# GpSimd's row scatters one stage later and its key scaling ahead of the first addition, in a gated delta-rule layer with a mixture of experts

## The chip, the cores and the metric

One core of a Trainium2 chip runs the whole program. The metric is the device time of one execution in microseconds (us). Three runs of the kernel before took 1393.51, 1395.70 and 1396.22 us; the median is 1395.7.

## The reference

Input is x of 2 sequences of 2048 tokens with 128 channels. What is computed:

```
h    = layernorm(x)
q, k, v = causal depthwise convolution of 4 taps over (h @ qkv_w.T)      8 heads of 128
beta, alpha = gates of h, one number per head and token
for each token t and head:  S = alpha_t * S
                            S = S + k_t (beta_t * (v_t - k_t S))
                            o_t = q_t S
x    = x + (rmsnorm(o) * norm_w * silu(h @ z_w.T)) @ out_w.T
h    = layernorm(x)
x    = x + sum over the 2 best of 8 experts of  weight * (relu(h @ W1 + b1) @ W2 + b2)
```

## The kernel before, in words

The 4096 tokens are cut into 16 groups of two chunks of 128 tokens. The recurrence is computed chunk by chunk: within a chunk a triangular system of 128 rows per head is solved, and a state S of 128 x 128 per head is carried from chunk to chunk.

The work is a software pipeline over the groups. A call `stages(g, a, par)` on every engine does three things interleaved: it prepares group a = g + 1 (projections, convolution, decays, the triangular solve), it finishes group g (the recurrence, the norm, the output product), and it routes group r = g - 1 to the experts (layernorm, the router's logits, the two best experts, a destination row for each token, and scatters of the rows to memory). There are 17 such stages: `stages(None, 0)`, `stages(0, 1)`, ... `stages(14, 15)`, `stages(15, None)`. Behind them the last group is routed by itself, and then 39 tiles of 256 rows go through the experts.

The order of the steps in a stage is written out by hand in one string, `ORDER` (lines 249 to 265). Every engine walks through the same list and issues, in that order, what is its own. An engine never goes ahead of its own next instruction, so the order of a step matters on the engine that has it, and there alone.

The steps that the change and the prediction touch:

- GpSimd (lines 587 to 659) has these steps in a stage: `diag.c` (line 629, the decay matrix of chunk c before its scan, beta on the diagonal), `last.n` (line 637, 16 of them, the last addition of the convolution of one 128-channel tile; 0 to 7 are the keys, 8 to 15 the queries), `ka.c` (line 620, the keys of group g scaled by their decay), `aq.c` (line 620, the same for the queries), `sp.c` (line 649, the state scaled), `nr` (lines 589 to 600, the normalised rows of group r are written into `rowbuf`) and `sc` (lines 601 to 611, four indirect DMAs that scatter `rowbuf` to the rows that `dest` names, in the memory tensor `rows_in`).
- `sc` waits for `dest` (VectorE, line 1132) and for `rowbuf`. `nr` of the next group waits for the landing of all earlier scatters, since it overwrites `rowbuf`, and for `rs` (VectorE, line 237, step `rms`).
- `diag.c` waits for the attention product of the same chunk of the group before (`at`, VectorE line 1170), which still reads the decay matrix. `last.n` waits for `first.n`, the two multiply-adds of VectorE (lines 1143 and 1146), which wait for `taps.n` of ScalarE (line 758), which waits for `proj.n` of TensorE and for `last.n-4`: the convolution has a ring of 4 buffers.
- `ka.c` waits for the decays' transfer, asked for in the stage before, and for the attention matrix `kq.c.1` of TensorE, which still reads the unscaled keys. TensorE's `ks.c` reads the scaled keys.
- TensorE's `kk.0.1` and `kk.1.u` (line 1553) need all 8 key tiles, so `last.7`. Their products (VectorE, `nm`, line 1162) go to memory (line 477), come back as 32 x 32 blocks (line 485, tile `blkN`), and are solved on VectorE by `inv.0` to `inv.21`: pairs of a product with two SBUF inputs (line 1056) and a reduction (line 1060), between them other steps of the stage. The solved blocks go out and in again (`to`, `ti`) and are merged by TensorE in the next stage.
- In `ORDER` the string begins with `... m.0.0 last.0 taps.3 ... first.3 ka.0 last.1 ...` and ends with `... g.1.0 last.15 kd.1.0 inv.13 rms.0 ... nr ... ps ... st.1.1 xs.1 tj sc`. Of GpSimd's steps the order is: `diag.0 last.0 ka.0 last.1 last.2 last.3 diag.1 last.4` to `last.7 sp.0 aq.0 ... ka.1 ... sp.1 last.15 nr sc`.

Of the kernel before, what the change touches and what calls it, by code (L numbers as in the profile page):

```python
# [6 lines left out]
def preln_delta_moe_kernel(nc, x_in, qkv_t, z_t, ab_t, conv_w, dt_bias, a_log, norm_w, out_t,  # L7
# [11 lines left out]
    NG = NCH // GC  # L19
# [27 lines left out]
    with ctx:  # L47
        ctx.enter_context(nc.allow_non_contiguous_dma("layout of blocks"))

        def sb(name, shape, dt=F32):  # L50
            return ctx.enter_context(nc.sbuf_tensor(name, shape, dt))
# [20 lines left out]
        taps = sb("taps", [128, NT, TAPS])  # L72
# [6 lines left out]
        kq = sb("kq", [128, 2, 2, H, GT])  # L79
# [7 lines left out]
        def part(i, k):  # L87
            n = GC * H * C
            return area[i][:, n * k:n * k + n].rearrange("p (g h c) -> p g h c", g=GC, h=H)
# [4 lines left out]
        kd = part(2, 0)  # L94
        squares, spare = part(2, 1)[:, 0], part(2, 1)[:, 1]
        R, zg = part(3, 0), part(3, 1)
# [13 lines left out]
        rhs = sb("rhs", [128, H, C])  # L110
# [116 lines left out]
        def rsqrt_step(s, v, y, t):  # L227
# [19 lines left out]
        RMS = 1 + RSQ  # L247
        RMS_PART = (0, 6, RMS)
        ORDER = """
            proj.0 proj.1 taps.0 taps.1 diag.0 first.0 v.0.0 proj.2 m.1.0 taps.2 al.0 first.1 proj.3 m.0.0 last.0 taps.3  # L250
            rdiag.0 me.1.0 v.0.1 first.2 proj.4 first.3 ka.0 last.1 me.0.0 m.1.1 taps.4 proj.5 me.1.1 ks.0.0 m.0.1 taps.5
            scan.0 first.4 m.1.2 proj.6 me.0.1 rdiag.1 ks.0.1 last.2 last.3 first.5 me.1.2 proj.7 m.0.2 m.1.3 al.1 taps.6
            diag.1 first.6 taps.7 last.4 proj.8 first.7 kk.0.0 me.0.2 me.1.3 m.0.3 last.5 proj.9 last.6 xl.0 rhs.0.0 me.0.3
            last.7 sp.0 scan.1 nm.0.0 taps.8 kk.0.1 u.0.0 taps.9 aq.0 nm.0.1 kk.1.0 first.8 last.8 nm.1.0 kk.1.1 nm.1.1
            proj.10 ue.0.0 rhs.0.1 taps.10 o.0.0 first.9 proj.11 first.10 proj.12 u.0.1 taps.11 first.11 taps.12 last.9
            sd.0.0 proj.13 ktr.0.0 ue.0.1 first.12 xl.1 aq.1 last.10 no.0 no.1 sq.0.0 proj.14 taps.13 last.11 st.0.0 ac.0
            sd.0.1 taps.14 g.0.0 o.0.1 first.13 ka.1 st.0.1 sq.0.1 proj.15 last.12 v.1.0 sm v.1.1 scale.0 bi ks.1.0 kd.0.0
            first.14 inv.0 taps.15 ks.1.1 last.13 rhs.1.0 inv.1 inv.2 last.14 inv.3 inv.4 first.15 rhs.1.1 u.1.0 inv.5
            kq.0.0 u.1.1 ue.1.0 g.0.1 inv.6 ue.1.1 o.1.0 o.1.1 ktr.0.1 sq.1.0 inv.7 s2 ac.1 sd.1.0 sp.1 sq.1.1 kd.0.1 inv.8
            scale.1 inv.9 inv.10 at.0.0 inv.11 ktr.1.0 inv.12 g.1.0 last.15 kd.1.0 inv.13 rms.0 inv.14 sd.1.1 ktr.1.1 kd.1.1  # L260
            rms.1 gn.0.0 kq.0.1 gn.0.1 gt.0.0 inv.15 at.0.1 z.0.0 inv.16 gt.0.1 gte.0.0 nr g.1.1 xt inv.17 gte.0.1 z.0.1
            zt.0.0 xe lg out.0 gn.1.0 zt.0.1 inv.18 rk gn.1.1 gt.1.0 inv.19 gt.1.1 x2.0 inv.20 gte.1.0 inv.21 kq.1.0 gte.1.1
            pf out.1 zg.0.0 z.1.0 tp zt.1.0 zg.0.1 ps st.1.0 z.1.1 zt.1.1 zg.1.0 zg.1.1 xs.0 x2.1 to at.1.0 kq.1.1 at.1.1 ti
            st.1.1 xs.1 tj sc
            """
        STEPS = [(name, *map(int, arg)) for name, *arg in (word.split(".") for word in ORDER.split())]

        def halves(b, c, u):

            return (b + 1) * HALVES + U * c + u + 1  # L270

        def chunks(b, c):

            return (b + 1) * GC + c + 1
# [5 lines left out]
        def tile(b, n):  # L280

            return (b + 1) * NT + n + 1
# [62 lines left out]
        def bc(ap, shape):  # L345
            return ap.to_broadcast(shape)
# [210 lines left out]
        def _(pool):  # L557
# [55 lines left out]
            def stages(g, a, par):  # L613

                def scale_by_decay(c, kind, done):

                    pool.wait_ge(acum_in[c], g * 16 + 16)
                    pool.wait_ge(kq_ready, halves(g, c, U - 1))
                    t = kq[:, 1 - par, kind, :, C * c:C * c + C]
                    nc.gpsimd.tensor_tensor(t, t, acum_b[:, c, :, :], ALU.mult).then_inc(done, 1)  # L620

                r = g - 1 if g is not None and not (isinstance(g, int) and g == 0) else None
                for step, *arg in STEPS:
                    if r is not None:
                        route(step, r, par)
                    if step == "diag" and a is not None:
                        c, = arg
                        pool.wait_ge(at_ready, halves(a, c, U - 1) - HALVES)
                        nc.gpsimd.tensor_tensor(  # L629
                            decay[:, c, :, :], bc(ident[:, :].rearrange("p (o c) -> p o c", o=1), [128, H, C]),  # L630
                            bc(beta[:, ds(a * GC + c, 1), :].rearrange("p o (h u) -> p (o h) u", u=1), [128, H, C]),
                            ALU.mult).then_inc(diag_ready, 1)
                    elif step == "last" and a is not None:
                        n, = arg
                        dst = (kT[par], qT[par])[n // H]
                        pool.wait_ge(conv_mid, tile(a, n))
                        nc.gpsimd.tensor_tensor(dst[:, n % H, :], tapA[:, n % RING, :], tapB[:, n % RING, :],  # L637
                                                ALU.add).then_inc(conv_done, 1)
                    elif step == "ka" and g is not None:
                        scale_by_decay(arg[0], 0, ka_ready)  # L640
                    elif step == "aq" and g is not None:
                        scale_by_decay(arg[0], 1, aq_ready)
                    elif step == "sp" and g is not None:

                        c, = arg
                        pool.wait_ge(scale_ready, chunks(g, c))
                        pool.wait_ge(S_ready, halves(g, c, U - 1) - U)
                        pool.wait_ge(o_mm, halves(g, c, U - 1) - U)
                        nc.gpsimd.tensor_tensor(S[:, 1 - c, :, :], S[:, c, :, :],
                                                bc(a_end[:, c, :].rearrange("p (h o) -> p h o", o=1), [128, H, C]),  # L650
                                                ALU.mult).then_inc(sp_ready, 1)

            stages(None, 0, 0)
            stages(0, 1, 1)
            for b in range(1, NG - 1):
                stages(b, b + 1, 1 - b % 2)
            stages(NG - 1, None, 0)
            for step in ROUTE_ORDER:
                route(step, NG - 1, 1)

# [1125 lines left out]
```

## Time and profile before

| | |
|---|---|
| median of 3 runs | 1395.7 us |
| the profiled execution | 1399.73 us, of it 1397.9 us span |
| busy share TensorE, VectorE, ScalarE, GpSimd | 86%, 83%, 60%, 51% |
| mean granted clock of TensorE | 0.965 of full speed |
| scatters of line 609 | 64, 64.6 us busy |
| GpSimd's idle time ahead of them | 202.1 us, of it 175.2 us until VectorE's `dest` |

The profile is of one execution. A span runs from the first to the last instruction. An instruction's row gives its start, its duration and, in brackets, the idle time of its engine before it with what ended that. Rows with xN merge N instructions in a row. The chain of waits follows the run back from its last instruction, at each step to what released it.

### The profile page before, as it was taken

How to read it: one execution, taken by the hardware profiler on the slowest of the kernel's cores; microseconds unless marked ns; L12 is line 12 of the kernel's file. 1: busy time of each engine (PE TensorE's matmuls, PEld its weight loads, DVE VectorE, ACT ScalarE, POOL GpSimd, SP SyncE). 2: the span in 40 equal slices, each digit the busy share in tenths (PEclk: the TensorE clock that was granted, in tenths of full speed). 3: DMA queues.
4: the chain of work that ended last, by engine and by line, in shares of the span. 5: the costliest groups of instructions: out<-in, count | busy, mean ns of one | idle time of the engine just before them, and what ended most of it. 6: DMA issues, size and time to landing. Idle time of an engine off the chain costs nothing.

```text
span 1397.9 us, 34191 instructions
## 1 busy us (share of the span) xinstructions
PE 1199.9 (86%) x12203; PEld 944.0 (68%) x12203; DVE 1164.4 (83%) x2531; ACT 832.0 (60%) x2536; POOL 707.9 (51%) x598
## 2 busy tenths in 40 slices
PE   0355999999999999999999999999999989479991
PEld 0233868686868687777777777777777767358881
DVE  6878898989898998989898989897989783578875
ACT  1252666666666666657566666756566655358884
POOL 3151727464555656473828292928192822235552
PEclk9997999999999999999999999999999998789996
DMA  6031212222221222131313141313121223432225
GB/s 208 0 98 32 73 35 73 47 69 62 54 63 53 62 54 64 52 68 48 84 34 91 28 98 25 103 28 88 30 85 43 73 55 98 104 96 78 76 65 181
DMA packets 163176, 97.10 MB, mean 69 GB/s; under 512 B 115623, under 2 KB 148269, under 8 KB 161988
## 3 DMA queue, kind: packets, MB, share of 16 engines
q1 hardware_dynamic: 124932, 82.25, 21.6%
q10 hardware_dynamic: 33536, 4.20, 2.1%
q0 software_dynamic: 4544, 8.47, 1.9%
q8 instruction: 102, 1.67, 0.5%
q14 instruction: 62, 0.51, 0.1%
HBM read 73.31 MB, written 24.61 MB: 70 GB/s over the span
## 4 chain that ended last, share of the span: by engine, by line
DVE 37%; PE 21%; POOL 17%; issue 10%; DMA 9%; SPq 3%; ACT 3%; POOLq 0%; DVEq 0%; ACTq 0%
DVE blkT L1060 9%; POOL kq L637 9%; DVE Y_sb L1056 9%; DMA blkN<-scr_n 4%; PE kx L1553 3%; POOL decay L629 3%; POOL rows_in L609 2%; DVE Gs L1204 2%; POOL kq L620 2%; DMA scr_n<-area 2%; PE rc L1717 2%; SPq L477 2%; DVE blkN L1047 1%; DVE area L1170 1%; DVE Y_sb L1043 1%
## 5 line engine op out<-in xcount | busy, mean ns | idle before, releaser
L637 POOL TENSOR_TENSOR kq<-tapA,area 128x256 f32<-128x256 f32 x256 | 252.0, 998 | 93.6 <-DVE area L1146 92.8
L758 ACT ACTIVATE area<-pj,taps 128x256 f32<-128x256 f32 x256 | 123.1, 481 | 142.7 <-PE pj L1567 136.5
L1056 DVE TENSOR_TENSOR Y_sb<-blkT,blkN 128x4 f32<-128x4 f32 (+18 forms) x304 | 169.5, 558 | 10.5
L609 POOL DMA_INDIRECT rows_in<-rowbuf,dest x64 | 64.6, 1009 | 202.1 <-DVE dest L1132 175.2
L1143 DVE SCALAR_TENSOR_TENSOR tapA<-pj,taps,tapA 128x256 f32<-128x256 f32 x256 | 122.2, 477 | 53.4 <-ACT tapA L758 51.6
L1553 PE MATMUL kx<-kq 128*128 128x128 f32 x1024 | 141.0, 285 | 20.0 <-ACT area L767 9.6
L1553 PEld LDWEIGHTS kx<-kq 128*128 128x128 f32 x1024 | 128.7, 197 | 38.4 <-issue 21.8
L620 POOL TENSOR_TENSOR kq<-kq,area 128x1024 f32<-128x1024 f32 x64 | 151.1, 2362 | 0.0
L1060 DVE TENSOR_REDUCE blkT<-Y_sb 128x2 f32<-128x4 f32 (+18 forms) x304 | 142.4, 469 | 5.2
L758 ACT ACTIVATE tapA<-pj,taps 128x256 f32<-128x256 f32 x256 | 123.0, 480 | 0.0
L1146 DVE SCALAR_TENSOR_TENSOR area<-pj,taps,area 128x256 f32<-128x256 f32 x256 | 121.4, 474 | 0.0
L666 POOL DMA_INDIRECT rows_out<-rhs,e_dst x78 | 78.1, 1001 | 69.7 <-DVE e_dst L1325 36.7
L594 POOL TENSOR_TENSOR rowbuf<-rowbuf,id_step 128x4 int32<-128x4 int32 x16 | 3.2, 198 | 201.5 <-DVE rs L237 198.5
L1640 PE MATMUL ob<-S,kq 128*128 128x128 f32 x512 | 101.7, 281 | 0.8 <-issue 0.7
L1641 PE MATMUL ob<-Us,area 128*128 128x128 f32 x512 | 100.0, 277 | 0.0
L836 ACT ACTIVATE Gs<-Gs,rs 128x128 f32<-128x128 f32 x256 | 79.9, 397 | 32.3 <-DVE rs L237 32.3
L1603 PE MATMUL rc<-w_hi,xn_hi 128*128 128x512 f16 x256 | 99.1, 387 | 0.0
L1604 PE MATMUL rc<-w_lo,xn_hi 128*128 128x512 f16 x256 | 98.8, 386 | 0.0
L1605 PE MATMUL rc<-w_hi,xn_lo 128*128 128x512 f16 x256 | 98.7, 385 | 0.0
L1154 DVE TENSOR_TENSOR_SCAN decay<-area,decay 128x1024 f32<-128x1024 f32 x32 | 93.0, 2906 | 0.0
L629 POOL TENSOR_TENSOR decay<-ident,beta 128x1024 f32<-128x1024 f32 x32 | 60.8, 1901 | 62.3 <-DVE w_lo L1012 35.0
L827 ACT ACTIVATE area<-ob 128x128 f32<-128x128 f32 x256 | 67.7, 288 | 40.6 <-PE ob L1641 40.6
(307 smaller groups left out, 3613.2 us busy)
## 6 DMA issues: line engine op xcount, KB each, us to landing
area<-scr_alpha SPq DMA_DIRECT2D x32, 512.0 KB, 4.2
area<-scr_acum SPq DMA_DIRECT2D x32, 512.0 KB, 4.0
blkN<-scr_n SPq DMA_DIRECT2D x32, 256.0 KB, 4.4
area<-rows_in SPq DMA_DIRECT2D x39, 130.0 KB, 2.3
scr_n<-area SPq DMA_DIRECT2D x128, 32.0 KB, 1.6
area<-rows_out SPq DMA_DIRECT2D x4, 1024.0 KB, 8.1
rows_in<-rows_in SPq DMA_DIRECT2D x8, 260.0 KB, 3.8
kq<-in_x SPq DMA_DIRECT2D x4, 512.0 KB, 6.2
```

The lines of the kernel that those rows point to most:

```text
L620: nc.gpsimd.tensor_tensor(t, t, acum_b[:, c, :, :], ALU.mult).then_inc(done, 1)
L629: nc.gpsimd.tensor_tensor(decay[:, c, :, :], bc(ident[:, :].rearrange("p (o c) -> p o c", o=1), [128, H, C]), bc(beta[:, ds(a * GC + c, 1) ...
L637: nc.gpsimd.tensor_tensor(dst[:, n % H, :], tapA[:, n % RING, :], tapB[:, n % RING, :], ALU.add).then_inc(conv_done, 1)
L758: ins = nc.scalar.activation(dst[:, n % RING, :], pj[n % 2][:, k:k + GT], ACT.Copy, scale=taps[:, t, k:k + 1])
L1056: ins = nc.vector.tensor_tensor(p4, bc(blkT[:, r0:, j:].rearrange("p r (o m) -> p r o m", o=1), [128, nr, w, wd]), bc(blkN[:, j:j + w, j:] ...
L1060: ins = nc.vector.tensor_reduce(blkT[:, r0:, j:j + w], p4, AX.X, ALU.add, negate=True)
L1143: nc.vector.scalar_tensor_tensor(out=tapA[:, n % RING, :], in0=pj[n % 2][:, 0:GT], scalar=taps[:, order[n], 0:1], in1=tapA[:, n % RING, :] ...
L1146: nc.vector.scalar_tensor_tensor(out=tapB[:, n % RING, :], in0=pj[n % 2][:, 2:2 + GT], scalar=taps[:, order[n], 2:3], in1=tapB[:, n % RING ...
L1553: ins = mm(o, lhs[:, hh, cs], rhs_[:, hh, cs], start=True, stop=True)
L1603: mm(rc[u][:, :], hi, wv_hi[:, k, w], start=(k == 0), stop=False)
L1640: mm(o, qT[1 - par][:, hh, C * c:C * c + C], S[:, c, hh, :], start=True, stop=False)
L1641: ins = mm(o, AT[:, c, hh, :], Us[:, hh, :], start=False, stop=True)
```

## The change

Two steps of GpSimd move in `ORDER`. `sc` moves from the end of the list to behind `last.15`, and there it scatters group r - 1, so each group's scatters go out one stage later than before. `ka.0` moves from behind `first.3`, where on GpSimd it follows `last.0`, to ahead of `last.0`, where it follows `diag.0`. All other steps keep their order, and no other engine has either step. Behind the last stage the scatters that are still to do are issued, and then the last group is routed as before. GpSimd's steps of a stage are now `diag.0 ka.0 last.0 last.1 ... last.15 sc nr`.

The string is broken into lines anew; cut to what moves:

```diff
-  ... first.1 proj.3 m.0.0 last.0 taps.3
-  rdiag.0 me.1.0 v.0.1 first.2 proj.4 first.3 ka.0 last.1 ...
+  ... first.1 proj.3 m.0.0 ka.0
+  last.0 taps.3 rdiag.0 me.1.0 v.0.1 first.2 proj.4 first.3 last.1 ...
...
-  scale.1 inv.9 inv.10 at.0.0 inv.11 ktr.1.0 inv.12 g.1.0 last.15 kd.1.0 inv.13 ...
+  scale.1 inv.9 inv.10 at.0.0 inv.11 ktr.1.0 inv.12 g.1.0 last.15 sc kd.1.0 inv.13 ...
...
-  st.1.1 xs.1 tj sc
+  ... st.1.1 xs.1 tj
...
                 for step, *arg in STEPS:
-                    if r is not None:
+                    if step == "sc" and r is not None and r > 0:
+                        route("sc", r - 1, par)
+                    elif step != "sc" and r is not None:
                         route(step, r, par)
...
             stages(NG - 1, None, 0)
+            route("sc", NG - 2, 1)
             for step in ROUTE_ORDER:
                 route(step, NG - 1, 1)
```

## Rows read from the trace of the kernel before

**Rows 1.** The page, part 4: the chain's shares of the span by engine.
```profile
DVE 37%; PE 21%; POOL 17%; issue 10%; DMA 9%; SPq 3%; ACT 3%; POOLq 0%; DVEq 0%; ACTq 0%
```

**Rows 2.** The chain in order of time: start us, us, what; seven of its pieces.
```profile
270.70 1.92 POOL decay L629
...
533.48 0.20 DVE dest L1132
...
539.45 1.92 POOL decay L629
...
542.05 2.29 POOL kq L620
...
552.40 2.64 POOL kq L637
...
600.53 0.20 DVE dest L1132
...
1013.25 1.91 POOL decay L629
```

**Rows 3.** GpSimd's timeline: start us, us, engine, line, operation, tiles, count [idle before].
```profile
520.99 1.47 POOL L597 TENSOR_SCALAR rowbuf<-xres,stat,rs 128x256 f32<-128x256 f32 x2
...
534.57 1.05 POOL L609 DMA_INDIRECT rows_in<-rowbuf,dest  x1 [12.11 <-DVE dest L1132]
...
573.97 0.73 POOL L637 TENSOR_TENSOR kq<-tapA,area 128x256 f32<-128x256 f32 x1 [1.72 <-DVE area L1146]
...
587.87 0.20 POOL L594 TENSOR_TENSOR rowbuf<-rowbuf,id_step 128x4 int32<-128x4 int32 x1 [13.17 <-DVE rs L237]
```

**Rows 4.** VectorE's timeline, the two early stages that have no scatters ahead.
```profile
121.17 1.85 DVE L1056 TENSOR_TENSOR Y_sb<-blkT,blkN 128x351 f32<-128x351 f32 x1
...
188.32 1.85 DVE L1056 TENSOR_TENSOR Y_sb<-blkT,blkN 128x351 f32<-128x351 f32 x1
...
201.41 0.68 DVE L1193 TENSOR_TENSOR S<-rc,S 128x512 f32<-128x512 f32 x1
...
222.86 0.69 DVE L1162 TENSOR_TENSOR area<-kx,decay 128x512 f32<-128x512 f32 x1 [0.20 <-PE kx L1553]
```

**Rows 5.** VectorE's timeline, one steady stage and the end of the solve before it.
```profile
522.04 0.68 DVE L1170 TENSOR_TENSOR area<-kx,decay 128x512 f32<-128x512 f32 x1
...
523.22 0.53 DVE L1056 TENSOR_TENSOR Y_sb<-blkT,blkN 128x351 f32<-128x351 f32 x1
...
524.80 0.63 DVE L1056 TENSOR_TENSOR Y_sb<-blkT,blkN 128x450 f32<-128x450 f32 x1
...
536.76 0.68 DVE L1193 TENSOR_TENSOR S<-rc,S 128x512 f32<-128x512 f32 x1
...
542.36 4.16 DVE L1154 TENSOR_TENSOR_SCAN decay<-area,decay 128x1024 f32<-128x1024 f32 x1
...
558.96 0.69 DVE L1162 TENSOR_TENSOR area<-kx,decay 128x512 f32<-128x512 f32 x1 [0.20 <-PE kx L1553]
```

**Rows 6.** GpSimd's timeline around the early stage that begins near 201.
```profile
187.89 1.90 POOL L629 TENSOR_TENSOR decay<-ident,beta 128x1024 f32<-128x1024 f32 x1 [15.07 <-DVE area L1170]
...
216.29 2.64 POOL L637 TENSOR_TENSOR kq<-tapA,area 128x256 f32<-128x256 f32 x1 [0.30 <-DVE area L1146]
```

**Rows 7.** Line 609 by itself: its 64 scatters from issue to landing.
```profile
DMA to landing us min/median/max: 2.5/4.0/5.4
```

**Rows 8.** Two lines of VectorE by themselves: duration ns min/median/max, first and last start.
```profile
L1344 DVE SCALAR_TENSOR_TENSOR area<-area x78: 674/688/693, 1236.6 to 1367.5; 128x512 f16<-128x512 f32 x78
...
L1154 DVE TENSOR_TENSOR_SCAN decay<-area,decay x32: 2277/2284/4310, 81.4 to 1095.1; 128x1024 f32<-128x1024 f32 x32
```

**Rows 9.** Timelines of VectorE and GpSimd in the expert stage, one moment.
```profile
1244.17 1.93 DVE L1293 TENSOR_TENSOR area<-Gs,GTs 128x992 f32<-128x992 f32 x1
...
1244.98 1.96 POOL L666 DMA_INDIRECT rows_out<-rhs,e_dst  x1 [1.12 <-ACT rhs L889]
```

**Rows 10.** Busy time in a stretch: PE, PEld, DVE, ACT, POOL, then PEclk, DMA, GB/s.
```profile
945.00:950.00 5.00, 5.00 (x47) 2.28 (x47) 4.97 (x6) 2.34 (x6) 5.00 (x4) 0.66 0.08 31
```

More of the change, by code:

```diff
@@ L249, in preln_delta_moe_kernel @@
         ORDER = """
[L250 to L263, printed above, removed]
@@ L264, in preln_delta_moe_kernel @@
-            st.1.1 xs.1 tj sc
-            """
+        proj.0 proj.1 taps.0 taps.1 diag.0 first.0 v.0.0 proj.2 m.1.0 taps.2 al.0 first.1 proj.3 m.0.0 ka.0
+        last.0 taps.3 rdiag.0 me.1.0 v.0.1 first.2 proj.4 first.3 last.1 me.0.0 m.1.1 taps.4 proj.5 me.1.1
+        ks.0.0 m.0.1 taps.5 scan.0 first.4 m.1.2 proj.6 me.0.1 rdiag.1 ks.0.1 last.2 last.3 first.5 me.1.2
+        proj.7 m.0.2 m.1.3 al.1 taps.6 diag.1 first.6 taps.7 last.4 proj.8 first.7 kk.0.0 me.0.2 me.1.3 m.0.3
+        last.5 proj.9 last.6 xl.0 rhs.0.0 me.0.3 last.7 sp.0 scan.1 nm.0.0 taps.8 kk.0.1 u.0.0 taps.9 aq.0
@@ new lines, in preln_delta_moe_kernel @@
+        nm.0.1 kk.1.0 first.8 last.8 nm.1.0 kk.1.1 nm.1.1 proj.10 ue.0.0 rhs.0.1 taps.10 o.0.0 first.9 proj.11
+        first.10 proj.12 u.0.1 taps.11 first.11 taps.12 last.9 sd.0.0 proj.13 ktr.0.0 ue.0.1 first.12 xl.1
+        aq.1 last.10 no.0 no.1 sq.0.0 proj.14 taps.13 last.11 st.0.0 ac.0 sd.0.1 taps.14 g.0.0 o.0.1 first.13
+        ka.1 st.0.1 sq.0.1 proj.15 last.12 v.1.0 sm v.1.1 scale.0 bi ks.1.0 kd.0.0 first.14 inv.0 taps.15
+        ks.1.1 last.13 rhs.1.0 inv.1 inv.2 last.14 inv.3 inv.4 first.15 rhs.1.1 u.1.0 inv.5 kq.0.0 u.1.1
@@ new lines, in preln_delta_moe_kernel @@
+        ue.1.0 g.0.1 inv.6 ue.1.1 o.1.0 o.1.1 ktr.0.1 sq.1.0 inv.7 s2 ac.1 sd.1.0 sp.1 sq.1.1 kd.0.1 inv.8
+        scale.1 inv.9 inv.10 at.0.0 inv.11 ktr.1.0 inv.12 g.1.0 last.15 sc kd.1.0 inv.13 rms.0 inv.14 sd.1.1
+        ktr.1.1 kd.1.1 rms.1 gn.0.0 kq.0.1 gn.0.1 gt.0.0 inv.15 at.0.1 z.0.0 inv.16 gt.0.1 gte.0.0 nr g.1.1 xt
+        inv.17 gte.0.1 z.0.1 zt.0.0 xe lg out.0 gn.1.0 zt.0.1 inv.18 rk gn.1.1 gt.1.0 inv.19 gt.1.1 x2.0
+        inv.20 gte.1.0 inv.21 kq.1.0 gte.1.1 pf out.1 zg.0.0 z.1.0 tp zt.1.0 zg.0.1 ps st.1.0 z.1.1 zt.1.1
@@ L266, in preln_delta_moe_kernel @@
+        zg.1.0 zg.1.1 xs.0 x2.1 to at.1.0 kq.1.1 at.1.1 ti st.1.1 xs.1 tj
+        """
         STEPS = [(name, *map(int, arg)) for name, *arg in (word.split(".") for word in ORDER.split())]
```

## The prediction, made before the change was run

> **What bounds the kernel now.** I read the chain of waits on the page first: VectorE holds the largest share, TensorE and GpSimd follow [rows 1]. Then the chain in order of time, to see where GpSimd stands in it. One steady stage runs from one write of `dest` to the next, 533.48 to 600.53, so 67.05 us. From `dest` the chain goes into GpSimd: the four scatters, `diag.0` (the decay product, line 629), `last.0`, `ka.0` (the key scaling, line 620), three more additions, `diag.1`, and at last `last.7`, which ends at 555.04 [rows 2]. The chain's times are those of the waits followed back, so a step's row may be shorter than the instruction. From there it goes to TensorE, to two DMAs and into the triangular solve on VectorE (lines 1056 and 1060), which ends just ahead of the next `dest`. The chain runs through `diag.0` in 11 of the 13 stage starts that have scatters ahead of them, the first at 270.70, the last at 1013.25 [rows 2].
>
> The timeline of GpSimd shows what it does meanwhile. It ends its last addition at 574.70, idles 13.17 us until the routing step `nr`, which VectorE's `rs` releases, works 1.7 us, and idles again 12.11 us until `dest` [rows 3]. So the change moves 4 scatters, `diag.0` and `ka.0` out of the chain and into these idle stretches. That is only half of it: what lies beside those stretches is VectorE in the middle of its solve, and that is the other half of the chain.
>
> **The change, part by part.**
>
> *The scatters leave the head of the stage.* The trace has this case: the stage that begins near 201 has no scatters ahead of it. I measure from the same VectorE instruction, the second state update (line 1193), to the same product (the last of line 1162). Without scatters that is 201.41 to 222.86, 21.45 us [rows 4]; with them 536.76 to 558.96, 22.20 us [rows 5]. The difference is 0.75 us, much less than the 5.77 us that the scatters hold between `dest` (533.68) and `diag.0` (539.45) [rows 2], because other things are late next. In the early stage `last.7` waits 0.30 us for VectorE's `first.7` and then takes 2.64 us [rows 6], as it does in the steady stage [rows 2]: a scan (line 1154) runs beside it. Removing GpSimd's backlog altogether gains no more than that, so I give `ka.0`'s earlier end nothing of its own: its key reader on TensorE comes after merges that did not wait for it. Ends of the gain: nothing, and 9.98 us (5.77 for the scatters, 1.92 for `diag.0`, 2.29 for `ka.0`) if nothing else were late. I take 0.75, the row of the same stretch without scatters. In the two scatter-headed starts where the chain came through a transfer instead I count none: 11 x 0.75 = 8.3 us.
>
> *The scatters in their new place.* They start when `last.15` ends (574.70). With the spacing of today (534.57 to the decay at 539.45, 1.2 us each) [rows 2, 3] issuing ends near 580 and the last lands at most 5.4 us later [rows 7], near 585. `nr` waits for the landing, and its other release is at 587.87 [rows 3]: hidden, with nearly 3 us to spare. VectorE does not pay: in the expert stage at the end two scatters go with each tile, and of the 78 two-input instructions of line 1344 none took over 0.693 us, the shortest 0.674 [rows 8]. The scatter itself can pay: one at 1244.98 took 1.96 us beside a two-input product that began at 1244.17, where the first of the stage here took 1.05 [rows 3, 9]. Four such would end issuing near 584 and land by 589.2, 1.3 us past the release; that is an upper bound, and I take nothing. The Trainium skill's page "SBUF — State Buffer", section "Who interferes with whom", says that a `tensor_tensor` does not starve the descriptor writing of such DMAs; by it the term is nothing, while the row at 1244.98 [rows 9] is against it, and keeps the bound.
>
> *`diag.0` now stands right behind `nr`.* `nr` ends at 522.46 [rows 3]; `diag.0` further waits only for the attention product that ends at 522.72 [rows 5]. This too is in the trace: in the two early stages `diag.0` was released by that same product (187.89, after 15.07 us of idling) [rows 6]. Beside it the solve's product of 351 elements took 1.85 us, both times [rows 4]; in the steady stage it takes 0.53 [rows 5]. VectorE waits until GpSimd's instruction is over. Price: 1.32 us at each start, on the solve. Nothing there covers it: VectorE shows no idle time from 522 to the end of the solve, and the products, the projections and the transfers of the next stage hang on its end.
>
> *`ka.0` now follows `diag.0` directly.* No row shows it there. That its instruction holds VectorE up is seen in the scan at 542.36: 4.16 us beside `ka.0`, against a median of 2.28 for line 1154 [rows 8], and it ends 2.18 us after `ka.0` (544.34), about what a scan alone takes [rows 2, 5]. So the waiting VectorE instruction goes before GpSimd's next one. Counted on: `diag.0` begins at about 522.8; the 351-element product ends 2.28 us later, as it did at 190.17 [rows 4, 6], at 525.08; `ka.0` runs from about 524.95 to 527.25. The product of 450 elements begins today 1.05 us after the 351-element one ends [rows 5], so it is ready at 526.13; it gets through from about 527.15, and ends 0.63 later at 527.8, not at 526.76: 1.04 us. Ends: nothing, if only instructions that do not wait fall beside it, and the whole 2.29. I take 1.04, between them, since the same product pattern is what `diag.0` met.
>
> *The sum.* 13 ordinary starts x (1.32 + 1.04) = 30.7. The two early starts have `diag.0` hidden already and pay `ka.0` alone: 2 x 1.04 = 2.1. The last group has no `diag.0`; `ka.0` comes right behind `nr`, so from 522.46 to 524.75 in the times of the steady stage; the 351-element product then ends near 525.2, not at 523.75: 1.4. Together 34.2, less 8.3: **+25.9 us**. The profiled execution took 1399.73 us (span 1397.9); it would take 1425.6. The median of the runs shown is 1395.7, 4.0 lower; the forecast on it is 1395.7 + 26 = **1422**.
>
> **Rivals.**
>
> *Only the gain is left (faster).* Place: the later part of the solve, where `diag.0` and `ka.0` now run. If VectorE's two-input products find the shared path free there, for instance because the longer idle stretch lets GpSimd finish ahead of them, the stall falls away. It decides where the stall is under 0.75 us a start. For it: `nr`'s own instructions at 520.99 stand beside the solve today without a stretched product. Against: those have one tensor input, and `diag.0` stalled VectorE both times it stood there [rows 4]. Time: 11 to 13 x 0.75 off, 1386 to 1387.
>
> *Stall and gain cancel (no change).* With half of the stall absorbed by waits that the trace shows as idle time of TensorE and ScalarE the sum is within a few us: 13 x 0.75 against 8.3. Against: VectorE itself is the one without idle time. Time 1396.
>
> *The landing takes the place of the old wait.* If the scatters reach 1.96 us each, `nr` is late by up to 1.3 us and routing with it, at 13 starts: up to 17 us more, 1439. For it one row [rows 9]; against it the 3 us to spare.
>
> *TensorE's clock falls more often.* In the 5 us from 945 the granted clock averaged 0.66, so part of it was at 1.2 GHz and the rest at 2.4 [rows 10]; that costs 5 x 0.34 = 1.7 us. The change leaves TensorE waiting some 2.4 us longer in each solve. If the clock fell at all 13 starts, 22 us more: 1444. Against: over the whole run the mean is 0.965 today.
>
> **How the numbers follow.** Forecast 0.68; clock 0.08; late landing 0.06; cancelling 0.05; only the gain 0.13. Slower by over 0.2% (2.8 us, about what a measurement of this kernel can tell from no change): 0.68 + 0.08 + 0.06 = 0.82; within it 0.05; faster 0.13. The forecast's own ends: low, `ka.0` costs nothing and the 1.32 remain, 13 x 1.32 - 8.3 = +9, 1405; high, `ka.0` costs its 2.29 whole at 13 + 3 starts, 13 x 1.32 + 16 x 2.29 - 8.3 = +45.5, 1441. That takes in the late landing; it leaves out the gain alone, cancelling, and part of the clock's case, about 0.2. Range 1404 to 1441.
>
> **What would show it.** Right: in a steady stage `diag.0` and `ka.0` stand directly behind `nr`; the solve's 351- and 450-element products are stretched (1.85, and about 1.7 us); scatters follow `last.15` at about 1.2 us each; `nr` is still released by `rs`; the first addition is released by VectorE's `first.0`; `dest` to `dest` is 68.7 us. Wrong: those products at 0.53 and 0.63, or `nr` released by the scatters' landing, or the stretch from line 1193 to the last of line 1162 shorter by well over 0.75 us, which would mean that GpSimd's head of stage was worth more than the early stage shows.

## The result, and the profile after

The changed kernel takes 1418.7 us (median of 4 runs, 1417.5 to 1420.7), beside 1396.0 us for the kernel before on the same chip: ratio 1.0165, 95% interval 1.0145 to 1.0186. It is 22.8 us slower by the medians, and the forecast was 26 us slower (1422). Its profiled execution has a span of 1418.8 us, 20.9 us over the 1397.9 of before, and the mean granted clock is 0.965 in both.

The chain's shares by engine, from the page (before: [rows 1]):

```profile
DVE 40%; PE 29%; issue 9%; DMA 9%; ACT 5%; POOL 5%; SPq 3%; ACTq 0%; POOLq 0%; DVEq 0%
```

The change does what it set out to do: GpSimd's share of the chain falls from 17% to 5%. On the chain the larger part of that goes to TensorE (21% to 29%) and the smaller to VectorE (37% to 40%): what GpSimd did at the head of a stage had other work beside it. What makes the run longer stands on VectorE, below. GpSimd's timeline over the stretch that answers to [rows 3] (start us, us, engine, line, operation, tiles, count, idle before and its releaser; line numbers are 1 to 3 higher than before on GpSimd and 4 higher on VectorE):

```profile
585.47 0.73 POOL L640 TENSOR_TENSOR kq<-tapA,area 128x256 f32<-128x256 f32 x1 [1.72 <-DVE area L1150]
586.35 1.05 POOL L610 DMA_INDIRECT rows_in<-rowbuf,dest  x1 [0.15 <-issue]
...
590.37 1.01 POOL L610 DMA_INDIRECT rows_in<-rowbuf,dest  x1 [0.30 <-issue]
599.41 0.20 POOL L595 TENSOR_TENSOR rowbuf<-rowbuf,id_step 128x4 int32<-128x4 int32 x1 [8.03 <-DVE rs L237]
599.58 1.47 POOL L598 TENSOR_SCALAR rowbuf<-xres,stat,rs 128x256 f32<-128x256 f32 x2
601.39 1.90 POOL L632 TENSOR_TENSOR decay<-ident,beta 128x1024 f32<-128x1024 f32 x1 [0.34 <-DVE area L1174]
603.24 2.65 POOL L621 TENSOR_TENSOR kq<-kq,area 128x1024 f32<-128x1024 f32 x1
619.43 1.51 POOL L640 TENSOR_TENSOR kq<-tapA,area 128x256 f32<-128x256 f32 x2 [13.54 <-DVE area L1150]
```

The scatters stand behind `last.15` and are issued by 591.4, `nr` is still released by VectorE's `rs` after 8.03 us of idling, `diag.0` and `ka.0` follow `nr` directly, and the next stage's first additions wait for VectorE alone. VectorE's timeline in the same stage, the end of the solve and the stretch from line 1197 (1193 before) to the last of line 1166 (1162 before):

```profile
600.12 0.58 DVE L1060 TENSOR_TENSOR Y_sb<-blkT,blkN 128x392 f32<-128x392 f32 x1
...
601.81 1.86 DVE L1060 TENSOR_TENSOR Y_sb<-blkT,blkN 128x351 f32<-128x351 f32 x1
...
604.73 1.65 DVE L1060 TENSOR_TENSOR Y_sb<-blkT,blkN 128x450 f32<-128x450 f32 x1
...
617.71 0.69 DVE L1197 TENSOR_TENSOR S<-rc,S 128x512 f32<-128x512 f32 x1
...
638.99 0.69 DVE L1166 TENSOR_TENSOR area<-kx,decay 128x512 f32<-128x512 f32 x1 [0.20 <-PE kx L1557]
```

`diag.0` holds the 351-element product up, 1.86 us for 0.53, and `ka.0` the 450-element one, 1.65 for 0.63 [rows 5]. The gain is there too: 617.71 to 638.99 is 21.28 us, beside 22.20 before [rows 5], so 0.92. The product of 392 elements, beside `nr`, is not stretched (0.58 us, 0.57 to 0.58 before).

The whole run in groups by line of VectorE (line, operation, count, then busy us and mean ns): the solve's products and the scan, first of the kernel before, then after.

```profile
L1056 DVE TENSOR_TENSOR Y_sb<-blkT,blkN 128x4 f32<-128x4 f32 (+18 forms) x304 | 169.5, 558 | 10.5
L1154 DVE TENSOR_TENSOR_SCAN decay<-area,decay 128x1024 f32<-128x1024 f32 x32 | 93.0, 2906 | 0.0
```

```profile
L1060 DVE TENSOR_TENSOR Y_sb<-blkT,blkN 128x4 f32<-128x4 f32 (+18 forms) x304 | 204.3, 672 | 10.5
L1158 DVE TENSOR_TENSOR_SCAN decay<-area,decay 128x1024 f32<-128x1024 f32 x32 | 73.2, 2286 | 0.0
```

The products cost 34.8 us more, and the two shapes of 351 and 450 elements alone account for 34.5 of it (18.7 and 15.7). The scans cost 19.8 us less, since `ka.0` no longer stands beside the first one, but the head of the stage has other waits behind it and gives back only some 0.9 us a start.

### The profile page after: what moved, and what is told of

It reads as the page before. It is cut to its first block, busy times and chain, and to the rows that moved or that the text cites. A ratio compares the mean times of both kernels' runs of the same rounds, so it can differ in the third digit from the quotient of the medians.

```text
span 1418.8 us, 34191 instructions
## 1 busy us (share of the span) xinstructions
PE 1197.7 (84%) x12203; PEld 944.3 (67%) x12203; DVE 1182.8 (83%) x2531; ACT 834.0 (59%) x2536; POOL 717.4 (51%) x598
## 4 chain that ended last, share of the span: by engine, by line
DVE 40%; PE 29%; issue 9%; DMA 9%; ACT 5%; POOL 5%; SPq 3%; ACTq 0%; POOLq 0%; DVEq 0%
DVE Y_sb L1060 10%; DVE blkT L1064 9%; POOL kq L640 4%; DMA blkN<-scr_n 3%; PE kx L1557 3%; DVE Gs L1208 2%; PE rc L1607 2%; DMA scr_t<-blkT 2%; DVE blkN L1051 2%; PE rc L1609 2%; PE rc L1608 2%; PE rc L1721 2%; DVE area L1150 1%; DVE area L1180 1%; DVE area L1174 1%
## 5 line engine op out<-in xcount | busy, mean ns | idle before, releaser
L1060 DVE TENSOR_TENSOR Y_sb<-blkT,blkN 128x4 f32<-128x4 f32 (+18 forms) x304 | 204.3, 672 | 10.5
L621 POOL TENSOR_TENSOR kq<-kq,area 128x1024 f32<-128x1024 f32 x64 | 155.3, 2428 | 0.0
L1064 DVE TENSOR_REDUCE blkT<-Y_sb 128x2 f32<-128x4 f32 (+18 forms) x304 | 142.5, 469 | 5.2
L787 ACT ACTIVATE area<-pj 128x512 f32<-128x512 f32 x64 | 38.1, 596 | 93.5 <-PE pj L1592 92.7
L1569 PE MATMUL pj<-xn_hi,w_hi 128*128 128x259 f16 x256 | 73.2, 286 | 17.7 <-DVE area L1150 9.7
```

Of the source, the lines that this page charges most:

```text
L1060: ins = nc.vector.tensor_tensor(p4, bc(blkT[:, r0:, j:].rearrange("p r (o m) -> p r o m", o=1), [128, nr, w, wd]), bc(blkN[:, j:j + w, j:] ...
L1064: ins = nc.vector.tensor_reduce(blkT[:, r0:, j:j + w], p4, AX.X, ALU.add, negate=True)
```

## The experiments

Three groups of kernels ran, each group on one chip beside the kernel before. That kernel took 1395.6 us beside the first four of the table below, 1402.7 beside `diag_scalar`, `ka_halves` and `held_solve`, and 1397.4 beside the last two, so kernels of different groups are compared by their ratios and by the shortest of their first 12 steady stages (one write of `dest` to the next), read from the profiles. The stages are the safer of the two. The kernel before was granted a mean clock of 0.965, 0.963 and 0.964 beside the three groups, while the kernels of the last two groups had 0.964 to 0.966, and where the kernel before runs slower on its chip the ratios beside it come out low: `held` and `held_solve` have the same ratio, though `held_solve` took 5.6 us more and its shortest stage is 0.50 us longer.

| kernel | median us | ratio to before, 95% interval | shortest stage, us |
|---|---|---|---|
| sc_only | 1400.8 | 1.0039 (1.0025 to 1.0053) | 67.44 |
| ka_only | 1418.3 | 1.0163 (1.0140 to 1.0186) | 68.28 |
| held | 1382.8 | 0.9907 (0.9885 to 0.9929) | 66.15 |
| sc_behind_ka | 1428.8 | 1.0240 (1.0215 to 1.0265) | 68.75 |
| diag_scalar | 1413.9 | 1.0085 (1.0058 to 1.0112) | 67.75 |
| ka_halves | 1408.9 | 1.0044 (1.0027 to 1.0061) | 67.78 |
| held_solve | 1388.4 | 0.9908 (0.9881 to 0.9935) | 66.65 |
| diag_eight | 1417.9 | 1.0148 (1.0123 to 1.0173) | 68.57 |
| held_sp | 1364.7 | 0.9778 (0.9752 to 0.9803) | 65.17 |
| before | 1395.6 | 1 | 67.03 |
| after (beside 1396.0) | 1418.7 | 1.0165 (1.0145 to 1.0186) | 68.49 |

**sc_only: the scatters move, the key scaling does not.** The edit is the kernel after with one step put back:

```diff
-  ... m.0.0 ka.0
-  last.0 taps.3 rdiag.0 me.1.0 v.0.1 first.2 proj.4 first.3 last.1 ...
+  ... m.0.0
+  last.0 taps.3 rdiag.0 me.1.0 v.0.1 first.2 proj.4 first.3 ka.0 last.1 ...
```

> The changed kernel with ka.0 back behind last.0: only the scatters are moved. Stall theory (VectorE's solve waits for GpSimd's two-input instructions that now stand beside it): diag.0 is still beside the solve, ka.0 is not. The 351-element product stays at 1.85 us, the 450-element one goes back to 0.63; 13 x 1.32 less 13 x 0.75 us, so +7 us on the kernel before (between +3 and +10). Rival, scatters in the wrong place (their descriptors or their landing beside the solve cost the time): the whole +23 us stays.

VectorE's timeline in one stage:

```profile
592.89 1.86 DVE L1060 TENSOR_TENSOR Y_sb<-blkT,blkN 128x351 f32<-128x351 f32 x1
...
595.81 0.63 DVE L1060 TENSOR_TENSOR Y_sb<-blkT,blkN 128x450 f32<-128x450 f32 x1
```

The kernel is 5.2 us slower than before, inside the +3 to +10 that was expected, with the 351-element product stretched in every stage and the 450-element one in none. Moving the scatters alone already puts `diag.0` beside the solve, and that stall (1.33 us) is more than the gain.

**ka_only: the key scaling moves, the scatters do not.** Here the edit is to the kernel before:

```diff
-  ... m.0.0 last.0 taps.3
-  rdiag.0 me.1.0 v.0.1 first.2 proj.4 first.3 ka.0 last.1 ...
+  ... m.0.0 ka.0 last.0 taps.3
+  rdiag.0 me.1.0 v.0.1 first.2 proj.4 first.3 last.1 ...
```

> The kernel before with ka.0 behind diag.0 and ahead of last.0, scatters left at the end of the stage. Stall theory: both stand behind the scatters and so behind the solve in the 13 ordinary starts; only the two early starts and none else pay, 1.0 to 1.5 us each, so +2 to +3 us on the kernel before, within what can be measured. Rival, the place of ka.0 ahead of the first addition itself costs time (the convolution starts 2.3 us later): 13 x up to 2.3, so up to +30 us.

My expectation was wrong by 20 us: this half alone costs 22.7 us, though in the steady stages neither product is stretched. The rival held. GpSimd's timeline behind the scatters:

```profile
547.84 1.93 POOL L629 TENSOR_TENSOR decay<-ident,beta 128x1024 f32<-128x1024 f32 x1
549.69 2.38 POOL L620 TENSOR_TENSOR kq<-kq,area 128x1024 f32<-128x1024 f32 x1
552.00 4.12 POOL L637 TENSOR_TENSOR kq<-tapA,area 128x256 f32<-128x256 f32 x3
```

ScalarE's row that waits for it, and then two of VectorE's timeline:

```profile
554.86 0.47 ACT L758 ACTIVATE area<-pj,taps 128x256 f32<-128x256 f32 x1 [3.56 <-POOL kq L637]
```

```profile
550.75 3.50 DVE L1154 TENSOR_TENSOR_SCAN decay<-area,decay 128x1024 f32<-128x1024 f32 x1
555.73 0.48 DVE L1143 SCALAR_TENSOR_TENSOR tapA<-pj,taps,tapA 128x256 f32<-128x256 f32 x1 [1.48 <-ACT tapA L758]
```

The same two instructions in a stage of the kernel before:

```profile
544.07 0.47 ACT L758 ACTIVATE area<-pj,taps 128x256 f32<-128x256 f32 x1 [1.35 <-PE pj L1567]
```

```profile
546.45 0.45 DVE L1143 SCALAR_TENSOR_TENSOR tapA<-pj,taps,tapA 128x256 f32<-128x256 f32 x1
```

With the scatters still ahead, `ka.0` pushes `last.0` to 552.00. ScalarE's `taps.4` needs the ring slot that `last.0` frees (the ring has four) and waits 3.56 us, where before it waited 1.35 us for TensorE, and VectorE's `first.4` waits 1.48 us for `taps.4`, where before it did not wait. This is read off the rows; no run with a longer ring tried it. The shortest stage grows by 1.25 us (67.03 to 68.28), 16 us over 13 stages, and the two early stages, where `ka.0` does stretch the 450-element product (2.10 and 1.65 us), pay 2.5. The two profiles lie 18.6 us apart, so that is about all of it; the medians lie 22.7 apart because the profiled execution of before, 1399.73 us, was itself 4 us over the median. The granted clock of `ka_only` was lower too, 0.957 to 0.961 in its five runs beside 0.960 to 0.969: in its profile it fell in five steady stages, of 69.20 to 71.06 us, where in the profile of before it fell in two; what that cost was not told apart. So the two halves are not worth what each costs alone: the step order has slack for `ka.0` ahead of `last.0` only once the scatters are gone from there.

**held: the kernel after, with `diag.0` kept out of the solve.** GpSimd waits, ahead of `diag.0`, for the solve's end and for `dest`:

```diff
+                        if c == 0:
+                            pool.wait_ge(inv_done, a + 1)
+                            if g is not None and g >= 2:
+                                pool.wait_ge(dest_done, routed(g - 2))
```

> The changed kernel with one wait more on GpSimd: diag.0 waits until the solve of the group before is done and the destinations of the group that is routed are written, so diag.0 and ka.0 run behind the solve and nothing is queued ahead of them but that wait. Scatters stay where the change put them. Stall theory: the 351- and 450-element products are back at 0.53 and 0.63 in every start, also in the two early ones; only the gain of 0.75 us a start is left, 13 x 0.75 and 2 x 1.3, so 8 to 13 us less than the kernel before, 1383 to 1388. Rival, scatters in the wrong place: still about +23 us. If the gain of 0.75 us is no gain: the same as before.

GpSimd's timeline in one stage:

```profile
595.85 1.90 POOL L636 TENSOR_TENSOR decay<-ident,beta 128x1024 f32<-128x1024 f32 x1 [11.39 <-DVE dest L1140]
...
600.51 1.51 POOL L644 TENSOR_TENSOR kq<-tapA,area 128x256 f32<-128x256 f32 x2 [0.44 <-DVE area L1154]
```

VectorE's two products in the same stage:

```profile
585.22 0.53 DVE L1064 TENSOR_TENSOR Y_sb<-blkT,blkN 128x351 f32<-128x351 f32 x1
...
586.81 0.63 DVE L1064 TENSOR_TENSOR Y_sb<-blkT,blkN 128x450 f32<-128x450 f32 x1
```

The kernel is 12.8 us faster than before and 36 us faster than after, with the same scatters and the same operations; GpSimd now idles 11.39 us ahead of `diag.0`. Both products are back at 0.53 and 0.63 us (the last group has no `diag.0` to hold: there `ka.0` still stretches the 351-element product, 1.95 us), and `last.0` still waits for VectorE. This is the gain of the change without its price: 67.03 to 66.15, so 0.88 us a stage.

**sc_behind_ka: diagonals and key scaling beside the solve, scatters at their old time.** The kernel after, with `sc` moved in the written order:

```diff
-  ... m.0.0 ka.0
+  ... m.0.0 ka.0 sc
   last.0 ...
...
-  ... g.1.0 last.15 sc kd.1.0 ...
+  ... g.1.0 last.15 kd.1.0 ...
```

> The changed kernel with the scatters moved to behind ka.0 at the head of the next stage, so they wait for the destinations as before and go out when they did before; diag.0 and ka.0 stay ahead of them, beside the solve. Stall theory: both products stretched as in the changed kernel, 13 x 2.36 and the early and last starts, and GpSimd's head of stage is 4.2 us shorter than before, which gains up to 0.75 us a start: +22 to +34 us on the kernel before. Rival, scatters in the wrong place: they are back, so no more than the time of the kernel before.

VectorE's two products in one stage, in which the scatters begin at 616.36:

```profile
602.65 1.86 DVE L1060 TENSOR_TENSOR Y_sb<-blkT,blkN 128x351 f32<-128x351 f32 x1
...
605.57 1.65 DVE L1060 TENSOR_TENSOR Y_sb<-blkT,blkN 128x450 f32<-128x450 f32 x1
```

The kernel is 33 us slower than before, as expected (+22 to +34). The products are at 1.86 and 1.65 us with the scatters nowhere near them, so it is not the scatters that hold VectorE. With the scatters back at the head of the stage a part of the gain goes as well: the two stalls on top of `held` would give 68.50 us, the shortest stage has 68.75, and by the mean of the 12 stages 0.6 of the 0.9 us that `held` gains is lost. Together with sc_only that settles which instruction has which price.

**held_solve: `diag.0` waits for the solve's end only.** Half of the hold above:

```diff
+                        if c == 0:
+                            pool.wait_ge(inv_done, a + 1)
```

> The kernel after the change, with the first group of diagonals waiting for the end of the triangular solve alone, not for the destinations' last operation too (that version took 1382.8 us). Theory: diagonals and key scaling stay clear of the 351- and the 450-element product (0.53 and 0.63 us), and what remains is that the diagonals run beside the small 128x4 product of the destinations and hold it some 0.3 to 1.3 us at a stage: 1383-1395 us, still no slower than before. Rival: the loss of the change hangs on where in the stage GpSimd's work stands and not on the two products: then the time stays between 1395 and 1419 us though they are short.

GpSimd's `diag.0`, and from VectorE's timeline the destinations' product beside it, which takes 0.18 us elsewhere:

```profile
595.24 1.90 POOL L634 TENSOR_TENSOR decay<-ident,beta 128x1024 f32<-128x1024 f32 x1 [9.56 <-DVE blkT L1066]
```

```profile
596.48 0.71 DVE L1133 TENSOR_TENSOR chosen<-chosen,place 128x32 f32<-128x32 f32 x1
```

`diag.0` ends at 597.14 and the small product at 597.19: it too waits the instruction out, 0.53 us more than it needs, and the shortest stage is 0.50 us over that of `held`. A stall goes by what is left of GpSimd's instruction, not by the size of VectorE's.

**ka_halves: the key scaling in two instructions.** The kernel after, with `ka.0` split by heads:

```diff
+                    if c == 0 and kind == 0:
+                        for u in range(U):
+                            hs = slice(HU * u, HU * u + HU)
+                            t = kq[:, 1 - par, kind, hs, C * c:C * c + C]
+                            ins = nc.gpsimd.tensor_tensor(t, t, acum_b[:, c, hs, :], ALU.mult)
+                        ins.then_inc(done, 1)
+                        return
```

> The kernel after the change, with the first key scaling split into two GpSimd instructions of four heads each (some 1.2 us apiece), against 1418.7 us after. Theory: the VectorE product waits until the GpSimd instruction that runs is over and then goes first. Then the 450-element product falls from 1.65 to 0.9-1.3 us, between the two halves, and the kernel to 1404-1414 us. Rival: GpSimd's second half gets in ahead of the waiting product: 1.65 to 1.75 us as now, kernel 1416-1422 us. Second rival: the scan or another two-input instruction behind meets the second half instead: product short, kernel still 1416-1422 us.

GpSimd's two halves, and VectorE's products of 450 and 406 elements, from the two timelines:

```profile
600.42 3.25 POOL L624 TENSOR_TENSOR kq<-kq,area 128x512 f32<-128x512 f32 x2
```

```profile
601.90 0.63 DVE L1067 TENSOR_TENSOR Y_sb<-blkT,blkN 128x450 f32<-128x450 f32 x1
...
603.22 0.88 DVE L1067 TENSOR_TENSOR Y_sb<-blkT,blkN 128x406 f32<-128x406 f32 x1
```

The 450-element product goes through whole between the two halves, and the second half waits instead: the two take 3.25 us, where one instruction over all heads takes 2.36 undisturbed. Only the 406-element product pays, 0.88 for 0.58. The stall falls from 1.02 to 0.30 us, and the shortest stage by 0.71. The product was ready as the first half ended and went ahead of the second, as the scan in [rows 5] suggested. The median of 1408.9 us lies in the expected range, which was written against 1418.7 us for the kernel after; at the ratio of 1.0044 it would be 1402 beside the 1396.0 of that run, 2 us under the range.

**diag_scalar and diag_eight: is it the second input, or the length?** Both are the kernel after with `diag.0` as eight instructions, one a head. In the first each has one tensor input and a column of `beta`, in the second two tensor inputs:

```diff
+                        if c == 0:
+                            for h in range(H):
+                                ins = nc.gpsimd.tensor_scalar(decay[:, c, h, :], ident[:, :],
+                                                              beta[:, a * GC + c, h:h + 1], None, ALU.mult)
+                            ins.then_inc(diag_ready, 1)
...
```

```diff
+                        if c == 0:
+                            for h in range(H):
+                                ins = nc.gpsimd.tensor_tensor(decay[:, c, h, :], ident[:, :],
+                                                              bc(beta[:, a * GC + c, h:h + 1], [128, C]), ALU.mult)
+                            ins.then_inc(diag_ready, 1)
...
```

> The kernel after the change, with the first group of diagonals written by eight one-input GpSimd instructions (the identity by one column of beta each) in place of one two-input one; times against 1395.6 us before and 1418.7 us after. Theory: VectorE's two-input products wait for GpSimd because GpSimd's instruction has two inputs too, as a one-input GpSimd instruction beside the 392-element product left that at 0.57 to 0.58 us. Then the 351-element product falls from 1.86 to 0.53-0.65 us and the kernel to 1395-1403 us (1.33 us less at 14 or 15 starts); if the key scaling then begins only behind the 450-element product, that falls to 0.63 too and the kernel goes to 1383-1392. Rival: any GpSimd instruction that reads or writes on-chip memory holds the product, one-input or not: the product is stretched still (1.3 us or more), kernel 1412-1424, or longer if eight instructions hold it one after the other.

> The kernel after the change, with the first group of diagonals written by eight two-input GpSimd instructions, one for each head; the control to the run with eight one-input ones, in which the 351-, 450- and 406-element products beside them took 0.52 to 0.63 us, unstretched. Theory (the second input makes the stall; VectorE waits for the end of the instruction that runs and then goes first): the products beside the eight are stretched, but each by no more than one short instruction: the 351-element product 0.60-0.95 us; a key scaling that comes later may hold another product. Stage 67.0-68.3 us by the profile, kernel 1397-1415 us where before takes 1395.6. Rival (what freed the products was that the instructions were short, not that they had one input): 0.53 us as beside the one-input ones, to within 0.03.

The timelines of GpSimd and VectorE with the one-input instructions:

```profile
603.15 5.63 POOL L634 TENSOR_SCALAR decay<-ident,beta 128x128 f32<-128x128 f32 x8 [0.35 <-DVE area L1180]
608.75 2.35 POOL L621 TENSOR_TENSOR kq<-kq,area 128x1024 f32<-128x1024 f32 x1
```

```profile
603.56 0.52 DVE L1066 TENSOR_TENSOR Y_sb<-blkT,blkN 128x351 f32<-128x351 f32 x1
...
609.40 2.25 DVE L1066 TENSOR_TENSOR Y_sb<-blkT,blkN 128x512 f32<-128x512 f32 x1
```

and with the two-input ones:

```profile
600.24 3.58 POOL L634 TENSOR_TENSOR decay<-ident,beta 128x128 f32<-128x128 f32 x8 [0.33 <-DVE area L1180]
603.78 2.36 POOL L621 TENSOR_TENSOR kq<-kq,area 128x1024 f32<-128x1024 f32 x1
```

```profile
600.66 0.72 DVE L1066 TENSOR_TENSOR Y_sb<-blkT,blkN 128x351 f32<-128x351 f32 x1
...
602.45 0.76 DVE L1066 TENSOR_TENSOR Y_sb<-blkT,blkN 128x450 f32<-128x450 f32 x1
...
603.90 2.68 DVE L1066 TENSOR_TENSOR Y_sb<-blkT,blkN 128x406 f32<-128x406 f32 x1
```

Beside the one-input instructions the 351-element product takes its own 0.52 us; beside short two-input ones 0.72, so 0.19 more. Shortness takes most of the stall away, one input all of it. Two products that met instructions with about as much left tell the two apart best: beside the two-input ones the 450-element product began with 0.27 us to go and lost 0.13; beside the one-input ones the 406-element product began with 0.28 us to go and lost nothing (0.58 us).

The contention is not gone with the one-input form: GpSimd bears it. Line 634 by itself in `diag_scalar` (duration ns min/median/max, first and last start):

```profile
L634 POOL TENSOR_SCALAR decay<-ident,beta x128: 588/602/1051, 75.6 to 1085.3; 128x128 f32<-128x128 f32 x128
```

In the stage shown, the three that began during, or just ahead of, VectorE's products of 351, 450 and 406 elements took 0.81, 1.05 and 0.80 us for 0.60.

Neither run gains what I expected from it, 1413.9 and 1417.9 us beside 1395 to 1403 and 1397 to 1415 (the ratio of `diag_scalar`, put on 1395.6, gives 1407.5, outside too), because eight instructions take longer (5.63 and 3.58 us) and push the long `ka.0` onto another product: the 512-element one, 2.25 for 0.69, and the 406-element one, 2.68 for 0.58. The stall moves with GpSimd's instruction.

**held_sp: the same lesson on another instruction.** The version `held`, with the second state scaling of a group (`sp.1`, beside the products that open the solve) in one-input form:

```diff
+                        if c == 1:
+                            for h in range(H):
+                                ins = nc.gpsimd.tensor_scalar(S[:, 1 - c, h, :], S[:, c, h, :],
+                                                              a_end[:, c, h:h + 1], None, ALU.mult)
+                            ins.then_inc(sp_ready, 1)
...
```

> The version with the held diagonals (1382.8 us beside 1395.6 before), in which the second state scaling of a group, on GpSimd at the start of the solve, is written as eight one-input instructions (a head's state by its column) instead of one two-input one; it leaves nothing out. Beside it the two 512-element products that open the solve take 0.92 and 1.68 us (medians; 0.69 at the least). Theory: both fall to 0.69-0.71 us, 1.2 us less at each of 14 stages, 17 us in all: 1361-1372 us, stage 64.8-65.2 us, the fastest of all. Rival 1: one-input GpSimd instructions hold VectorE as well: the two products stay or grow, 1380-1400 us. Rival 2: the scaling now takes some 5.6 us in place of 2.35, holds back the last addition and the scatters behind it, and that comes out at the end of the stage: products short, but 1375-1390 us.

It is the fastest of all, 1364.7 us, 2.2% under the kernel before. The groups of the second of VectorE's two opening products and of the solve's first one behind it, each shape apart, in `held` and then here:

```profile
L1055 DVE TENSOR_TENSOR blkN<-blkN,Y_sb 128x512 f32<-128x512 f32 x16 | 26.5, 1658 | 0.5
...
L1064 DVE TENSOR_TENSOR Y_sb<-blkT,blkN 128x4 f32<-128x4 f32 x16 | 12.4, 772 | 0.5
```

```profile
L1061 DVE TENSOR_TENSOR blkN<-blkN,Y_sb 128x512 f32<-128x512 f32 x16 | 14.7, 918 | 0.5
...
L1070 DVE TENSOR_TENSOR Y_sb<-blkT,blkN 128x4 f32<-128x4 f32 x16 | 2.6, 163 | 0.6
```

The second opening product gives back 11.8 us and the 4-element product behind it 9.8: in `held` `sp.1` stretched the one or the other, stage by stage. The span falls by 18.5 us (1380.8 to 1362.3). The time is as expected, but not my split of it: the first opening product did not shrink (14.6 to 14.4 us), the 4-element product had not been counted, and neither had `last.15`, which now follows `sp.1` later and lets the 64-element product go (7.3 us less) to stretch the one of 144 or 196 instead (4.0 more). A further 5.8 us were lost on three small products beside the eight instructions, told of at the end.

## Why the prediction was right, and where a size was off

**The stalls.** This was the main term: 34.2 us forecast (30.7 + 2.1 + 1.4), and the group of the solve's products grew by 34.8. `diag.0` cost 1.33 us a start (1.32 forecast), `ka.0` 1.02 (1.04). The last group's 351-element product took 1.95 us, 1.42 more than its 0.53 (1.4 forecast). Only the first of the early starts missed: its 450-element product took 2.10 us, 1.47 more instead of 1.04. The working has `ka.0` start 2.15 us behind the start of `diag.0` and take 2.29 us; it started 1.85 behind and took 2.65 (603.24 in the rows above), because it in turn waited for the 351-element product. The two slips cancel, and it ends where the prediction had it. Taken from `held`, where neither stall is there, the terms add up stage by stage:

| kernel | stalls on top of the 66.15 us of `held` | sum | shortest stage measured |
|---|---|---|---|
| sc_only | `diag.0` 1.33 | 67.48 | 67.44 |
| after | `diag.0` 1.33, `ka.0` 1.02 | 68.50 | 68.49 |
| ka_halves | `diag.0` 1.33, second half 0.30 | 67.78 | 67.78 |
| diag_scalar | `ka.0` on the 512-element product 1.56 | 67.71 | 67.75 |
| diag_eight | 0.19 and 0.13, `ka.0` on the 406-element product 2.10 | 68.57 | 68.57 |
| held_solve | `diag.0` on the destinations 0.53 | 66.68 | 66.65 |
| sc_behind_ka | `diag.0` 1.33, `ka.0` 1.02, and the scatters ahead of `last.0` | 68.50 without the scatters | 68.75 |

Each stall is one row of VectorE against the length that the same product has undisturbed. That the first six sums come out to within 0.05 us is the strongest evidence here that nothing covers these stalls. By the mean of the 12 stages in place of the shortest they come out to within 0.2 us, but for `diag_scalar`, whose mean is 0.4 over its sum; it has one stage of 70.78 us in which the granted clock fell to 0.65 for 4 us.

**The gain at the head of the stage** was mis-sized: "13 ordinary starts" carried the price, but only 11 x 0.75 = 8.3 us were counted as gain. The span rose by 20.9 us where the products rose by 34.8 (and the two that open the solve by 1.4 more), so some 15.3 us came back. Of it 13 x 0.88 = 11.4 is the gain that `held` shows; the early stage, from which I took 0.75, was a little low, and the two starts that the chain passed by gain as well. The rest, some 4 us, lies in longer stages: over the shortest one the 13 steady stages add 8.3 us in the profile before and 4.1 after. Most of the 8.3 is in two stages of the kernel before, 69.49 and 69.86 us long, in which the granted clock fell:

```profile
946.00:950.00 4.00, 4.00 (x21) 1.53 (x14) 4.00 (x5) 1.79 (x5) 4.00 (x3) 0.57 0.03 11
1082.00:1086.00 4.00, 4.00 (x43) 1.92 (x42) 3.97 (x6) 2.34 (x6) 4.00 (x4) 0.59 0.08 29
```

(Busy time of before in 4 us each; the third number from the right is the clock, between the levels of 1.2 and 2.4 GHz.) The steady stages of the profile after have no such stretch. So this part of the gain looks like that execution's clock rather than the change; it was read off, not tried.

**The scatters in their new place** cost nothing, as taken. The first took 1.05 us and they follow each other at some 1.3 us (1.2 forecast). Line 610 by itself:

```profile
DMA to landing us min/median/max: 2.3/2.4/5.6
```

The last one starts at 590.37, so even at 5.6 us it has landed by 596, and `nr` starts at 599.41. The bound from [rows 9], 1.96 us each, did not come about: the four took 0.97 to 1.08 us with the solve's products of 100 to 324 elements beside them, and over the run those products cost 0.2 us more than before. That `tensor_tensor` does not starve descriptor writing, as the Trainium skill's page "SBUF — State Buffer", section "Who interferes with whom", has it, agrees with these four scatters. Why the one of [rows 9] took 1.96 us stays open.

**The rivals.** "Only the gain is left" did not happen as the change stands. `held`, which takes the stalls away by a wait, shows what the gain alone is worth: the rival gave 1386 to 1387 us, `held` took 1382.8. Late landing and cancelling fell with the rows above. The clock's rival fell too: the mean is 0.965 in both, and the clock did not fall in the steady stages after.

**What I got wrong** came later, in the expectation for ka_only: I gave the early `ka.0` a price of a few us where it cost 22.7, because I looked at the stall it would no longer make, and not at the ring slot that `last.0` frees behind it.

## What to carry to other kernels

Idle time on GpSimd is not free room if VectorE runs two-input work on its bounding path meanwhile: price a moved GpSimd instruction by the VectorE instruction that it will stand beside, which waits until GpSimd's is over. A long two-input GpSimd instruction belongs where VectorE reads on-chip memory once (the solve's reductions, one input each, cost 142.4 us before and 142.5 after, with `ka.0` now beside one of them) or waits itself; failing that, cut it into pieces or write it with one tensor input, which takes longer, and look which instruction the next long one then meets. And try the halves of a change apart before believing that they add: here one half alone cost 5 us, the other alone 23, both together 23, and both with a wait added gained 13.

## What the runs showed of the hardware

A two-input VectorE product that begins while a two-input GpSimd instruction runs waits for it in every run, and the size of the wait follows one rule: it is 0.13 to 0.15 us less than what is left of GpSimd's instruction when the product begins. In the stages shown 1.47 us left cost 1.33 (`after`, 351 elements), 1.16 cost 1.02 (450), 2.24 cost 2.10 (`diag_eight`, 406), 0.66 cost 0.53 (`held_solve`, 32) and 0.27 cost 0.13 (`diag_eight`, 450). The Trainium skill's page "SBUF — State Buffer", section "Who interferes with whom", says that a VectorE instruction with two inputs in SBUF contends with a GpSimd instruction that reads SBUF. For GpSimd's two-input instructions every run agrees.

For its one-input ones I expected nothing, and for VectorE's time that holds at the diagonals (0.52 us beside them, 0.53 without) and beside `nr` (0.58 and 0.57 us for the 392-element product). But they do contend, and GpSimd pays: up to 1.05 us for 0.60 at the diagonals, and 0.93 for 0.55 for the second of `nr`'s two scalings, beside the 392-element product, in the kernel before as well. By the rule above, as an estimate, the three products beside the one-input diagonals would have lost 0.05, 0.43 and 0.14 us; they lost nothing. VectorE does not go free everywhere. In `held_sp`, with eight one-input instructions from 556.59 to 561.87, three small products of the solve took longer than in `held`: 16 elements 0.24 for 0.17 us, and these two, 0.36 for 0.20 and 0.43 for 0.26:

```profile
556.59 5.28 POOL L658 TENSOR_SCALAR S<-S,a_end 128x128 f32<-128x128 f32 x8
```

```profile
559.00 0.36 DVE L1070 TENSOR_TENSOR Y_sb<-blkT,blkN 128x36 f32<-128x36 f32 x1
...
561.31 0.43 DVE L1070 TENSOR_TENSOR Y_sb<-blkT,blkN 128x100 f32<-128x100 f32 x1
```

Why these are stretched and the products beside the diagonals are not stays open; no run told it apart. I had also not expected how exactly the two engines take turns: in `ka_halves` VectorE's 450-element product, ready as the first half ended, went ahead of GpSimd's second half in the 14 stages that follow the first (0.63 us; 1.02 in the first).
